# Two transformer layers in one kernel: the cross scores in row groups, and the end of layer 1 in another order

## The reference, cut to what matters

```python
h = _ln(x) * (1 + sc_msa) + sh_msa
x = x + _self_attn(h, ...) * g_msa            # windows of 64 tokens, shifted by 32
h = _ln(x) * (1 + sc_mca) + sh_mca
q = (h @ w_q + b_q).reshape(B, L, H, D)       # H = 16 heads of D = 8
scores = einsum('bqhd,bkhd->bhqk', q, k) / sqrt(D)   # 77 context keys
top_s, top_i = top_k(scores, 16)
attn = softmax(top_s); o = sum of attn * v at top_i
x = x + (o @ w_co + b_co) * g_mca
h = _ln(x) * (1 + sc_mlp) + sh_mlp
u = h @ w_m1 + b_m1; a, b = u[..., :512], u[..., 512:]
x = x + ((silu(a) * b) @ w_m2 + b_m2) * g_mlp
```

## Time and profile before

| | before |
|---|---|
| median of 3 runs | 457.19 us (456.02 to 457.80) |
| the profiled execution | 457.88 us, its span (first to last instruction) 456.1 us |
| busy share of the span | PE 79%, DVE 67%, ACT 44%, POOL 24% |
| mean granted TensorE clock | 0.862 |

### The profile page before, as it was taken

One profiled execution on the slowest core, in us unless ns is written; L12 is line 12 of the kernel. 1 busy time (PEld: TensorE's weight loads), 2 busy tenths in 40 slices (PEclk: granted clock), 3 DMA queues, 4 the chain that ended last, 5 costly groups with the idle time before them and its releaser, 6 DMA issues.

```text
span 456.1 us, 8978 instructions
## 1 busy us (share of the span) xinstructions
PE 360.9 (79%) x3320; PEld 214.0 (47%) x3320; DVE 304.4 (67%) x1288; ACT 201.5 (44%) x300; POOL 110.5 (24%) x136
## 2 busy tenths in 40 slices
PE   0858999999989978899978889767584566675885
PEld 0736323233333156677655467653363344454464
DVE  4386978999996065666238362245989999997342
ACT  1141037766647835666531114322453455654411
POOL 8045500004420021001025100021443544444020
PEclk9988559999999998999999575767877877776999
DMA  7326141113000000000000000000000000000000
GB/s 199 72 92 184 35 135 54 54 55 87 3 1 3 0 1 2 1 2 1 0 1 2 5 1 7 4 1 1 1 1 1 1 2 1 1 1 1 0 24 25
DMA packets 10811, 12.16 MB, mean 27 GB/s; under 512 B 2378, under 2 KB 9103, under 8 KB 10767
## 3 DMA queue, kind: packets, MB, share of 16 engines
q1 hardware_dynamic: 10469, 11.55, 8.9%
q0 software_dynamic: 256, 0.01, 0.0%
q10 hardware_dynamic: 42, 0.01, 0.0%
HBM read 8.69 MB, written 2.62 MB: 25 GB/s over the span
## 4 chain that ended last, share of the span: by engine, by line
PE 55%; DVE 29%; ACT 7%; issue 5%; POOL 1%; DMA 1%; SPq 1%; ACTq 0%; DVEq 0%
PE psum L1366 6%; PE psum L1426 5%; PE psum L1394 5%; PE psum L1379 5%; DVE left L1196 4%; DVE left L1203 4%; DVE mx L1141 4%; PE psum L1528 3%; DVE top L1193 3%; PE psum L1267 3%; DVE top L1200 3%; PE psum L1437 3%; PE psum L1465 2%; PE psum L1409 2%; PE psum L1495 2%
## 5 line engine op out<-in xcount | busy, mean ns | idle before, releaser
L1141 DVE TENSOR_REDUCE mx<-psum 128x1 f32<-128x512 f32 x128 | 80.2, 681 | 8.2 <-PE psum L1366 8.1
L742 ACT ACTIVATE big<-psum 128x1024 f32<-128x1024 f32 x64 | 62.3, 1022 | 39.4 <-PE psum L1379 39.1
L1366 PE MATMUL psum<-KS,QS 72*128 72x512 bf16 x128 | 50.5, 429 | 4.4 <-DVE mx L1141 3.6
L1426 PE MATMUL psum<-kblk,qf 128*128 128x308 f32 x128 | 46.6, 496 | 1.1 <-DVE qf L1074 0.8
L566 POOL TENSOR_TENSOR rstd<-vareps,minus_half 128x4 f32<-128x4 f32 x12 | 12.2, 1020 | 145.5 <-DVE vareps L912 145.4
L1437 PE MATMUL psum<-ident,pr 128*77 128x128 f32 x256 | 39.3, 304 | 10.3 <-POOL pr L683 10.3
L1437 PEld LDWEIGHTS psum<-ident,pr 128*77 128x77 f32 x256 | 35.1, 170 | 18.3 <-POOL pr L683 13.8
L1379 PE MATMUL psum<-QS,KS 75*128 75x512 bf16 x128 | 39.6, 397 | 0.4
L683 POOL TENSOR_TENSOR pr<-pr,early 128x616 f32<-128x616 f32 x16 | 23.9, 1492 | 55.9 <-ACT early L852 35.0
L1394 PE MATMUL psum<-big,V 128*9 128x512 f32 x256 | 34.3, 609 | 0.5 <-ACT big L742 0.5
L1366 PEld LDWEIGHTS psum<-KS,QS 72*128 72x128 bf16 x128 | 11.8, 102 | 46.0 <-DVE mx L1141 24.2
(11 more groups left out here) (198 smaller groups left out, 656.5 us busy)
## 6 DMA issues: line engine op xcount, KB each, us to landing
QS<-scr_q SPq DMA_DIRECT2D x8, 288.0 KB
KS<-scr_k SPq DMA_DIRECT2D x8, 288.0 KB
scr_q<-qp SPq DMA_DIRECT2D x2, 384.0 KB, 2.7
scr_k<-kp SPq DMA_DIRECT2D x2, 384.0 KB, 3.3
early<-in_L_xcond_w_ada_dram SPq DMA_DIRECT2D x1, 576.0 KB, 9.8
wmlp<-in_L_xcond_W_mlp_dram SPq DMA_DIRECT2D x2, 256.0 KB, 3.7
scr_k<-kp SPq DMA_DIRECT2D x2, 256.0 KB, 3.5
wm<-in_L_xcond_w_m_dram SPq DMA_DIRECT2D x1, 512.0 KB, 4.1
```

The lines of the kernel that those rows point to most:

```text
L742: freed(act.activation(pT[:, u % 2, 1024 * half:1024 * (half + 1)], ps, ACT.Exp), "sT", 0, u, half)
L1141: freed(dve.tensor_reduce(mx[:, n % 3, NT * hh + q:NT * hh + q + 1], ps, AX_X, ALU.max), "max", t, q)
L1366: filled(pe.matmul(ps, QS[b][0:ROWS, h, q * P:(q + 1) * P], KS[b][0:ROWS, h, :], start=True, stop=True), "max", j, q)
L1426: last = pe.matmul(ps[:, 512 * a:512 * a + HH // 2 * S], qf[:, b, i * P:(i + 1) * P], kb[:, c0:c0 + HH // 2 * S], start=True, stop=True)
```

## The change

1. Scores of both layers' cross attention: `kown` holds each key row once per head slot of 4 (4 x 77 columns), and a product contracts over the 32 rows of its 4 heads alone, so that the two products of a half stand in two row groups of the array and write two banks. GpSimd builds 2 tensors of 616 columns, one for each layer and both early, in place of 4 of 1232.
2. Layer 1 is written from one list of items, `ORDER`, which all engines walk through; each takes the items that concern it (an item with `<` is TensorE's place alone, the one with `>` the other engines'). Batch 0's turn and projection come earlier among the window units, the scores of a half always take room W0, and batch 0's MLP chunks stand one a half in halves 11 to 14.
3. Batch 0's silu is written as z + z tanh(z) with z = (a + bias)/2: ScalarE writes tanh and z, GpSimd multiplies and adds (`swish`), VectorE does the rest as before. `a` and `b` of a chunk are one room.
4. Batch 1's end is done for its first three tiles and then for its last one (`TILES`); the stores of the last part are split between SyncE and ScalarE.

The diff, cut:

```diff
+ORDER = """
...
+    K9 Q11 p400< A10 p400> s500 S500 B10 d10 T9 C10 n500 D10 V4< t500<
+    K10 V4> t500> Q12 m000< U4< A11 B11 m000> d11 w000 N500 T10 C11 U4> D11 g000
...
+TILES = [(0, NT), (0, NT - 1), (NT - 1, 1)]
...
+        elif kind == "Q":
+            topk = True
+            use("W0", "sc", 1, at[0])
...
+        elif kind == "m":
+            use("W" if last else "W1", "m", *at)
+        elif kind == "r":
+            use("M1", "out", *part_key(5, *at))
...
-        kblk = sb("kblk", [P, B, H, S])
+        kown = sb("kown", [P, 2, B, G, S])
...
-            for b in range(B):
-                wait_read(sp, "out", 5, b)
-                sp.dma_start(out[b, SHIFT:SHIFT + (NT - 1) * P, :].rearrange("(i p) c -> p i c", p=P),
...
+            store(sp, 0, 0)
+            store(sp, 1, 1)
+            store(sp, 1, 2, first=True)
+            sp.wait_ge(s_out, 16 * OUT_DMAS)
...
-            def ctx_blocks(layer):
...
+            def own_keys():
+                pool.wait_ge(s_mask4, 1)
+                for l2 in range(2):
+                    wait_read(pool, "kc", l2)
+                    pool.tensor_tensor(kown[:, l2, :, :, :], kcT[:, l2, :, :].unsqueeze(2).broadcast_to([P, B, G, S]),
+                                       mask4[:, :].unsqueeze(1).unsqueeze(3).broadcast_to([P, B, G, S]), ALU.mult)
...
+            def swish(b, c):
+                pool.wait_ge(s_half, c + 1)
+                pool.tensor_tensor(sa[b][c % 2], sa[b][c % 2], gT[:, b, c, :], ALU.mult).then_inc(s_swish, 1)
+                pool.wait_ge(s_swish, 2 * c + 1)
+                pool.tensor_tensor(gT[:, b, c, :], sa[b][c % 2], gT[:, b, c, :], ALU.add).then_inc(s_swish, 1)
...
+            def silu_out(b, p, c):
...
+                if b == 0:
+                    if c >= 2:
+                        act.wait_ge(s_swish, 2 * (c - 1))
+                    act.activation(sa[0][c % 2], ps, ACT.Tanh, scale=0.5, bias=half_b[:, c:c + 1])
+                    act.activation(gT[:, 0, c, :], ps, ACT.Identity, scale=0.5, bias=half_b[:, c:c + 1])\
+                        .then_inc(s_half, 1)
+                else:
...
+                    act.activation(sa[b][c % 2][:, own], ps, ACT.Silu, bias=cols[:, v:v + 1]).then_inc(s_silu, 1)
...
+            def gate_mul(b, p, c):
...
+                if b == 0:
+                    dve.wait_ge(s_swish, 2 * (c + 1))
+                    swished = gT[:, 0, c, :]
...
-                    last = pe.matmul(ps[:, 512 * a:512 * a + HH // 2 * S], qf[:, b, i * P:(i + 1) * P],
-                                     kb[:, c0:c0 + HH // 2 * S], start=True, stop=True)
+                    r = 2 * (e % 2) + a
+                    rows = slice(QUAD * r, QUAD * (r + 1))
+                    last = pe.matmul(ps[:, 512 * a:512 * a + G * S], qf[rows, b, i * P:(i + 1) * P], kb[rows, :],
+                                     start=True, stop=True)
...
+            def mlp_in_pair(b, p, c):
...
+                for n in range(2):
+                    at = n * HID + c * P
+                    last = pe.matmul(ps[:, n * N + i0 * P:n * N + (i0 + ni) * P], W["wm1"][:, at:at + P], hT[:, b, own],
+                                     start=True, stop=True)
+                filled(last, "m", b, p, c)
```

More of the change, by code:

```diff
@@ new lines, in rooms_in_turns @@
+    for e in range(-1, HALVES + 3):
+        if e + 1 < HALVES:
+            use("W", "sc", 0, e + 1)
+        if 1 <= e <= HALVES:
+            for part in range(2):
+                use("X", "pT", 0, e - 1, part)
+        if e % 2 == 0 and 1 <= e // 2 <= B * NT:
+            use("M0", "pvc", 0, e // 2 - 1)
+        if e % 2 == 0 and e >= 4:
+            use("M1", "pvcT", 0, e // 2 - 2)
+        for at, key in ((ARRIVE["oT"], ("oT", 0, 1)), (ARRIVE["out"], ("out", 0, 1)),
+                        (ARRIVE["lnT"], ("lnT", 1, 1)), (ARRIVE["qc"], ("qc", 0, 1)),
+                        (11, ("oT", 1, 0)), (13, ("out", 1, 0)), (15, ("lnT", 2, 0))):
+            if e == at:
+                use("M1", *key)
+        if e > HALVES:
+            for c in (0, 1) if e == HALVES + 1 else (2, 3):
+                use("X", "mlp", 0, 0, c)
@@ L668, in _, with difference @@
                 add_bias(3, b)
[L669 to L673 removed]
+            def difference(e):
                 k = e % 2
@@ L894, in _ @@
+            store(act, 1, 2, first=False)
         @block.vector
@@ new lines, in window_pairs @@
+                    for j in range(2):
+                        for w in range(2):
+                            t0, q0 = i * P + w * WIN, QUAD * (2 * half + j)
+                            last = pe.matmul(ps[w * WIN:(w + 1) * WIN, j, c * WIN:(c + 1) * WIN],
+                                             stationary[q0:q0 + QUAD, b, at[0](c), t0:t0 + WIN],
+                                             moving[q0:q0 + QUAD, b, at[1](c), t0:t0 + WIN], start=True, stop=True)
+                return last
@@ new lines, in window_pv @@
+            def window_pv(u):
+                b, i = steps[u]
+                ps = open_room(pe, "pv", 1, u)
+                if i == 0:
+                    wait_read(pe, "qkv", 1, b, "v")
+                for half in range(2):
+                    wait_read(pe, "sT", 1, u, half)
+                for h in range(H):
+                    c, j = divmod(h, NQ)
+                    p0 = HALF * j + WIN * c
+                    last = pe.matmul(ps[QUAD * j:QUAD * j + 2 * DV, c * WIN:(c + 1) * WIN],
+                                     VW[:, b, i, h, :, :].rearrange("p w e -> p (w e)"),
+                                     pT[:, u % 2, p0:p0 + WIN], start=True, stop=True)
+                filled(last, "pv", 1, u)
```

1310 lines of the change are left out of this document (667 added, 643 removed).

## The result

The changed kernel takes 461.81 us (median of 4 executions), the kernel before 456.61 beside it; the ratio is 1.0098, 95% interval [1.0053, 1.0143]. It is slower by 1%, and the forecast of 441 is 21 us off, outside its range. (Executions of these kernels fall in two levels; the ratios here take those of the faster level alone, and the traces of e1, e5, e6, e8 and e10 are of executions of the slower one.) The profiled execution took 461.09 us, its span 459.4, with a mean granted clock of 0.816 against 0.862 before.

The account below looks back on a forecast made before the run. Four stretches had different limits: TensorE (layer 0), batch 0's road to its first scores (window units), VectorE (top-16 halves), a dependent sequence (end). Terms -4.5 - 3.5 + 8.5 - 17.0 = -16.5 gave 441 us, range 435 to 450.

Parts of the forecast that it names:

- Term 1: Layer 0's cross attention: score products in two row groups overlap, 0.55 us for 1.04, nine pieces; -4.5 us (0 to -5.2).
- the rival of strict order: Score products: passes run strictly in written order, three pass lengths left of four, gain halved to -2.3; 444 us, chance 0.06.
- The reading from the 64-column passes of rows 4: Window scores: 64 passes took 1.06 us, so at least three ran together and two row groups should run two at a time.
- Term 2: Window units: earlier turn and projection (2.8 less 0.7 us) and shorter first scores (1.2); -3.5 us, bounds -1 and -5.
- Term 3: Top-16 halves: VectorE's added work less a removed wait, +3.2, and new waits, 5.3; +8.5 us, bounds +3.9 and +18.5.
- the chunk loop: Top-16 halves: one turn of a batch 0 MLP chunk through VectorE, TensorE, ScalarE and GpSimd takes 7.05 us.
- Term 4: The end, from VectorE's last top-16 step: 23.2 us for 40.2, -17.0 (-13 at the low clock for most of it).
- The shared port: Top-16 halves: GpSimd's 8 new operations each halt VectorE for 1.25 us; 451 us, chance 0.05.
- TensorE stays at 1.2 GHz: Low clock where the chunk loop needs TensorE: +10 us in the top-16 halves, +3 at the end; 454 us, chance 0.13.

Follow-up runs that it names:

- e1: The changed kernel with the old score products over all 128 rows in both layers; 449.3 us, ratio 0.9823 to the kernel before.
- e5: The changed kernel with each pair of layer 0's row-group score products issued twice into the same room; 471.1 us median.
- e6: e1 with layer 0's score products writing only the first half of their columns (154 of 308); 446.8 us.
- e8: e1 with batch 0's MLP chunks and output product moved behind the last top-16 half; 463.1 us, ratio 1.0084.
- e10: e1 with three moves in the list: batch 1's queries copied one place later, its first turn written ahead of the MLP chunk; 450.1 us.
- e2: The changed kernel with the old score products in layer 0 alone, layer 1's in row groups; 453.9 us, ratio 0.9926.
- e4: The kernel before with nothing of the change but both layers' scores in row groups; 462.7 us, ratio 1.0130.
- e7: e1 with layer 1's old score products issued twice into the same room; 452.4 us, ratio 0.9897.
- e9: e3 with both halves of a layer 0 tile's scores written together, four products in four row groups; 453.1 us, ratio 0.9891.
- e13: The same kernel as e10, timed again in five rounds; 449.5 us, ratio 0.9811.
- e3: The changed kernel with the old score products in layer 1 alone, layer 0's in row groups; 455.9 us, ratio 0.9972.
- e11: e9 and e10 together: four row groups in layer 0 and the three moves in the list; 450.3 us, ratio 0.9864.

## Why the prediction was wrong

**Term 1, the step that failed.** "two row groups should run two at a time: 0.55 us in place of 1.04, a gain of 0.49" priced only the length of a product and took the granted clock of the earlier trace rows, 0.97, as given. Two things were wrong in it, of very different size. The small one: the pair takes 0.72 us at the full clock. By a pass of 0.26 us, three lengths are 0.78 and two 0.52, so the rival of strict order was nearer than my value. The Trainium skill ("TensorE: Matmul & The Clock Gate", Packing small matmuls) has that order as a rule; for the pair the trace nearly agrees, 0.72 against the 0.78 worked out from it. For four groups it doesn't: strict order with two adjacent passes a product would take five lengths, 1.3 us, and eight passes took 0.73. The reading from the 64-column passes of rows 4 was thus right for four groups and wrong for two. The large one: 24 us of layer 0 at 0.50, 7.3 us of score stretch in place of -4.5, shown by e2 and e4, which differ from after and from before in the products and the build of their keys alone. I had the low clock as a rival only for layer 1, "the change takes work off it", and even there as a matter of how much work TensorE has. e7 shows that the amount counts there (0.79 to 0.90 with more of it); for layer 0, e6 and after's gap-free hole show that it isn't the amount alone.

Even at the full clock the gain would have been small. The chain of the earlier trace rows has one score piece a tile, so -0.49 for nine pieces looked sound, but e9, with 0.31 less at that piece, brought tiles from 5.75 to 5.60 apart, as the transposes behind it took 0.15 more. And the sentence that ScalarE "is not near the new period" looked at its sum alone: in the chain of before 3.1 of a tile's 5.75 us are ScalarE's, between the rows shown.

**Term 2** came out at -8.2 for -3.5, beyond its own bound of -5, and by luck: most of it is not the list's. After's chain, against the earlier trace rows:

```profile
299.76 1.09 PE psum L1401 x8
300.85 1.57 PE psum L1580 x62
302.42 2.01 PE psum L1415 x8
...
312.60 0.81 PE psum L1544 x4
```

The turn is 5.6 us late, the projection 3.6, though layer 1 began 9 late. The clock of the window units was 0.77 in place of 0.64, and 1.6 us are the first scores (0.81 for 2.44, both in those rows). e4, which has nothing of the list, shows how little the list had to do with it. From layer 1's first window product to the first MAX8:

| trace | first product | first MAX8 | us |
|---|---|---|---|
| before | 245.75 | 313.24 | 67.5 |
| e4, list as before | 253.17 | 313.94 | 60.8 |
| after | 254.89 | 314.15 | 59.3 |
| e1 | 249.11 | 313.75 | 64.6 |
| e13 | 248.13 | 308.19 | 60.1 |
| e6 | 244.30 | 302.33 | 58.0 |

e4 has 6.7 of the 8.2 us. The last three run the same instructions there and lie 6.6 us apart; the clock of the 90 us ahead of the first MAX8 was 0.74 in before and e1, 0.81 in e13, 0.83 in e6, 0.84 in e4 and 0.85 in after. So the clock that one execution happened to have is worth more here than the list, of whose 2.8 - 0.7 us no run shows anything clear of that.

**Term 3** was right for what the change adds (10.65 forecast, 10.7 between e8 and e1), though partly by luck: of the 5.3 us of waits 3.6 were to be at the chunks and 1.7 at batch 0's last residual, and e1 and e3 have 5.1 at the chunks and none at the residual. It was right for the chunk loop, 7.05 forecast. In after the loop is the distance of the L1215 rows of the timeline:

```profile
402.51 0.75 DVE L1215 SCALAR_TENSOR_TENSOR big<-psum,cols,big 128x512 f32<-128x512 f32 x1 [0.97 <-POOL big L751]
...
403.41 3.62 PE L1637 MATMUL psum<-hT,wm 128*128 128x512 f32 x4 [2.16 <-DVE big L1215]
...
411.14 0.75 DVE L1215 SCALAR_TENSOR_TENSOR big<-psum,cols,big 128x512 f32<-128x512 f32 x1 [2.31 <-POOL big L751]
...
412.03 1.96 PE L1637 MATMUL psum<-hT,wm 128*128 128x512 f32 x4 [0.96 <-DVE big L1215]
...
418.08 0.75 DVE L1215 SCALAR_TENSOR_TENSOR big<-psum,cols,big 128x512 f32<-128x512 f32 x1
```

8.6 us with the products at the low clock (3.62), 6.9 with them at the high one (1.96). The stage came out longer by what I had not looked for: 2.1 us of VectorE for the projected queries, 3.1 at divisions whose turn TensorE now writes behind a chunk's products (both by e3's rows), and in after the low clock, 2.7 more than e1's 115.6. The wait of 1.7 for batch 0's last residual didn't come in these traces; e6, e7 and e9 have it with 2.6.

**Term 4** was right at the clock it was worked out for: 23.2 forecast, 23.0 in e10 at 1.00. At 0.78 it is 27.0. The half microsecond allowed for the low clock was too little, the 4 us of the bound (-13) about right.

**The chances.** The shared port played no part that shows: VectorE's busy time in the stage grew by 5.3 us (99.31 to 104.61), what its new work was priced at. The time lies beyond "TensorE stays at 1.2 GHz", 454 us, because that rival was confined to layer 1. A change that swaps the form of a product in a stretch at 0.97 could have lost all of that clock. What that costs could have been estimated from twice's durations; it came to 3.6 us a tile (9.37 less 5.75), for as many tiles as it lasts.

## What to carry to other kernels

When products are made narrower so that they can run side by side, price the granted clock of the whole stretch before the passes: here 0.3 us less a pair at the full clock came with 7.3 us more of a stretch that TensorE bounds. If row groups are used, try all four at once (eight passes then took what four had, and the clock stayed down for a shorter time), but even that was no faster here than the old form. Print the whole chain between two pieces that you mean to shorten, and see what stands there besides them. Of a change in several parts, time the parts: here one that cost 12.5 us hid a gain of 1.8%. And where the clock of one and the same code moves a stretch by 6.6 us from execution to execution, one trace of each kernel can't credit a change with a few microseconds.

## What the runs showed of the hardware

TensorE busy without a gap stayed at the lower level for 24 us while pairs of 32-row score products stood in its stream (after, e3, e4); before, with scores over 128 rows, the same stretch was at 1.00. Half as many columns at full height left 190 to 210 us at 0.99 behind a fall of some 3 us, and all four row groups filled together had falls of 3 (e9) and 7 us (e11) in place of the 24. Two 32-row products of 308 columns in two row groups took 0.72 us at the full clock, four in four row groups 0.73, two over 128 rows 1.04. Doubling the narrow ones gave executions between 455.6 and 479.9 us of one and the same kernel.
